# Token rows that hold the last 64 normalised channels once

## The reference

```
h = concat(patches @ W.T + b, txt)           # (32, 274, 192)
h = h + attention(layernorm(h))              # 12 heads of 16, rope, causal
x = layernorm(h)
route_c, route_u = argmax(softmax(x @ Wsc)), argmax(softmax(x @ Wsu))
out = h + ffn_common[route_c](x) + dropped * ffn_unique[route_u](x)
```

## Time and profile before

| | |
|---|---|
| median of 3 runs | 1414.29 us (1412.52 to 1417.49) |
| profiled execution | 1427.62 us, of which span 1425.9 us |
| attention phase | to about 925 us of the span |
| expert phase | from there, 44 tiles |
| busy in the span | PE 1234.0 us, PEld 1049.4, DVE 906.9, ACT 560.0, POOL 628.5 |
| moved | 177.93 MB, mean 125 GB/s |

### The profile page before, as it was taken

One profiled execution on the slowest core, in us unless ns is written; L12 is line 12 of the kernel. 1 busy time (PEld: TensorE's weight loads), 2 busy tenths in 40 slices (PEclk: granted clock), 3 DMA queues, 4 the chain that ended last, 5 costly groups with the idle time before them and its releaser, 6 DMA issues.

```text
span 1425.9 us, 33277 instructions
## 1 busy us (share of the span) xinstructions
PE 1234.0 (87%) x12722; PEld 1049.4 (74%) x12722; DVE 906.9 (64%) x2063; ACT 560.0 (39%) x959; POOL 628.5 (44%) x996
## 2 busy tenths in 40 slices
PE   6889999999999999999999987468995788889874
PEld 4667777777777777777777775367994787789874
DVE  5676776786787777787777874567873343445331
ACT  1234334434444344344344343133552344455430
POOL 4133333334534534534534525415325465455564
PEclk8899999999999999999999998579996899889987
DMA  6001211213323313213323223477764566657530
GB/s 204 20 20 48 69 39 58 63 58 100 111 60 107 106 58 111 99 61 104 108 59 106 86 61 109 144 292 271 254 236 126 168 213 208 220 207 271 203 127 26
DMA packets 84368, 177.93 MB, mean 125 GB/s; under 512 B 16446, under 2 KB 57701, under 8 KB 84208
## 3 DMA queue, kind: packets, MB, share of 16 engines
q1 hardware_dynamic: 70544, 146.93, 31.8%
q0 software_dynamic: 13664, 28.84, 5.7%
HBM read 129.15 MB, written 50.38 MB: 126 GB/s over the span
## 4 chain that ended last, share of the span: by engine, by line
PE 41%; DVE 21%; issue 15%; POOL 11%; ACT 6%; DMA 3%; another core or an unknown queue 1%; SPq 1%; POOLq 0%; DVEq 0%; ACTq 0%
PE y_ps L1629 9%; PE h_ps L1618 9%; DVE capped L971 4%; ACT PT L739 3%; PE round_banks L582 3%; PE gen L502 3%; POOL sorted_d L226 3%; DVE xn L987 3%; POOL PT L853 3%; PE gen L544 2%; PE round_banks L555 2%; DVE nm L975 2%; PE gen L511 2%; DVE nm L973 2%; PE gen L594 2%
## 5 line engine op out<-in xcount | busy, mean ns | idle before, releaser
L739 ACT ACTIVATE PT<-round_banks 128x1752 f32<-128x1752 f32 x96 | 156.7, 1632 | 176.0 <-PE round_banks L582 176.0
L853 POOL TENSOR_SCALAR_AFFINE_SELECT PT<-PT 128x512 f32<-128x512 f32 x192 | 118.1, 640 | 209.8 <-ACT PT L739 209.3
L1708 ACT ACTIVATE Gl<-h_ps,W 128x256 f32<-128x256 f32 x264 | 118.1, 474 | 233.1 <-PE h_ps L1618 147.8
L1618 PE MATMUL h_ps<-XH,Wh 128*128 128x256 f32 x528 | 155.4, 310 | 46.7 <-issue 29.9
L1629 PE MATMUL y_ps<-W,Gl 128*128 128x192 f32 x1056 | 193.2, 338 | 2.8 <-issue 2.8
L1629 PEld LDWEIGHTS y_ps<-W,Gl 128*128 128x128 f32 x1056 | 181.5, 199 | 4.9 <-issue 4.8
L1533 POOL DMA_INDIRECT out_dram<-Y,sid x88 | 95.5, 1085 | 154.3 <-DVE Y L1801 130.8
L502 PE MATMUL gen<-w_emb,xT 128*128 128x192 f32 (+1 forms) x768 | 142.9, 338 | 7.7 <-DMA ident<-in_ident_dram 7.7
L1618 PEld LDWEIGHTS h_ps<-XH,Wh 128*128 128x128 f32 x528 | 109.2, 207 | 50.9 <-issue 37.4
L1618 PE MATMUL h_ps<-XH,Wl 128*128 128x256 f32 x528 | 146.6, 297 | 0.0
L971 DVE TENSOR_TENSOR capped<-round_banks,masks_f 128x1024 f32<-128x1024 f32 x96 | 116.2, 1211 | 33.7 <-PE round_banks L555 33.7
(11 more groups left out here) (272 smaller groups left out, 2462.5 us busy)
## 6 DMA issues: line engine op xcount, KB each, us to landing
W<-in_experts_dram SPq DMA_DIRECT2D x44, 771.0 KB
W<-in_experts_dram SPq DMA_DIRECT2D x44, 672.0 KB
xT<-in_xT_dram SPq DMA_DIRECT2D x32, 591.0 KB
X<-sorted_d SPq DMA_DIRECT2D x35, 450.0 KB
stage<-rows_d SPq DMA_DIRECT2D x64, 224.0 KB
rows_d<-xn SPq DMA_DIRECT2D x32, 256.0 KB
rows_d<-h SPq DMA_DIRECT2D x32, 192.0 KB
out_dram<-h SPq DMA_DIRECT2D x32, 192.0 KB
```

The costliest lines, as they stand in the source:

```text
L739: act.activation(PT[(JG * b + j) % 2][:], R[:, :, 0:438], ACT.Exp, scale=SCALE).then_inc(exps, 1)
L853: pool.affine_select(x[:, :, at:at + P], x[:, :, at:at + P], [[0, GH], [1, P]], ALU.is_ge, 0.0, base=0, channel_multiplier=-1)
L1618: mm = pe.matmul(h_ps[f % 3][:, 0:ROWS], w[t.par][:, cols], x, start=(k == 0), stop=(k == len(products) - 1))
L1708: act.activation(Gl[t.par][:, f, :], h_ps[f % 3][:, 0:ROWS], ACT.Gelu, bias=W[t.i][:, B1O + f:B1O + f + 1]).then_inc(g_ready, 1)
```

## The change

The row of `rows_d` and `sorted_d` holds the 192 normalised channels once, 1544 bytes in all. VectorE writes them with one scaling per tile. In the expert phase TensorE turns columns 0 to 127 and then 64 to 191, so the second half of `xt_ps` has channels 64 to 127 in lanes 0 to 63 and channels 128 to 191 in lanes 64 to 127. ScalarE rounds all of it as before. VectorE takes the rest of lanes 64 to 127 and writes it to lanes 0 to 63 of XH, over the channels that are not needed. The high part is now in the upper lanes and the low part in the lower ones; the weights, being stored twice, are unchanged.

```diff
-DX = 2 * P
+DX = D
...
-            def scale_twice(which, k, dst, src):
-
-                scale(which, k, dst[:, 0:P], src[:, 0:P])
-                twice = lambda x: x.rearrange("p (a d) -> p a d", d=D - P)
-                return scale(which, k, twice(dst[:, P:DX]), twice(src[:, P:D]).broadcast_to([P, 2, D - P]))
...
-                    scale_twice(LN2, 0, xn2[b % 2][:, 0, :], h[b % 8][:, 0, :])
-                    scale_twice(LN2, 1, xn2[b % 2][:, 1, :], h[b % 8][:, 1, :]).then_inc(xn2_ready, 1)
+                    scale(LN2, 0, xn2[b % 2][:, 0, :], h[b % 8][:, 0, :])
+                    scale(LN2, 1, xn2[b % 2][:, 1, :], h[b % 8][:, 1, :]).then_inc(xn2_ready, 1)
...
-                    scale_twice(LN2T, 0, xn2t[:], ht[g % 4][:]).then_inc(xn2t_ready, 1)
+                    scale(LN2T, 0, xn2t[:], ht[g % 4][:]).then_inc(xn2t_ready, 1)
...
-                    mm = pe.transpose(xt_ps[:, ROWS + k * P:ROWS + (k + 1) * P],
-                                      x[:, k, P:DX], eye[:])
+                    mm = pe.transpose(xt_ps[:, ROWS + k * P:ROWS + (k + 1) * P], x[:, k, D - P:D], eye[:])
...
-                low, cols = slice(D - P, P), slice(ROWS, 2 * ROWS)
-                dve.tensor_tensor(XH[t.par][low, cols], xt_ps[low, cols], XH[t.par][low, cols], ALU.subtract).then_inc(xt_ready, 1)
+                low, high, cols = slice(0, D - P), slice(D - P, P), slice(ROWS, 2 * ROWS)
+                dve.tensor_tensor(XH[t.par][low, cols], xt_ps[high, cols], XH[t.par][high, cols], ALU.subtract).then_inc(xt_ready, 1)
```

## The result

The changed kernel took 1409.65 us (median of 20 runs, 1394.36 to 1420.93) against 1418.97 us before (20 runs, 1412.32 to 1426.71). The ratio is 0.9919, with a 95% interval of 0.9891 to 0.9947: 0.81% or 11.5 us faster, by the interval 7.5 to 15.5 us. The two medians are 9.3 us apart, and so are the means of all twenty; 11.5 us is the upper reading of the gain. The forecast was 1409.2 us, but it stood on three runs of before with a median of 1414.29 us, 4.7 us under that of the twenty. So the time was met partly by luck; what has to be judged is the difference. Forecast were 5.1 us, and measured were 9.3 or 11.5, about twice as much.

A forecast was written before the change was run, and what follows sets the result against it. TensorE was taken to bound the attention phase, VectorE's chain of waits the first 65 us of the expert phase. 3.5 + 1.1 + 0.5 = 5.1 us off 1414.29 gave 1409.2 us, range 1402 to 1418.

The forecast's parts named there:

- The fourth turns: Attention turns 8, 12 to 32, scalings beside GpSimd's selects: 0.5 us saved in each of seven, 3.5 us.
- The last turns: End of attention phase, no new batch: two lone scaling groups save 0.50 and 0.44 us, the tail 0.2; 1.1 us.
- The bytes: Four chained transfers between the phases, 13.5 us: rows of 1544 instead of 1800 bytes save 0.5 us.
- Covered after all: Rival, 21%: in attention, another wait replaces TensorE's 0.89 us and transfers are pure latency; gain 0 to 2.5 us, 1413 us.
- Fewer pauses: Rival, 16%: in the tile loop, 64 KB less per tile removes one or two pauses of 6.3 us; 1403 us.
- Other pauses: Rival, 16%: VectorE's program, 72 instructions shorter, shifts tile-loop pauses; slower from two more on, 1421.8 us.
- A second pass: Rival, 5%: L1770's write across lanes in the expert phase takes 850 ns, not 427; +5.6 us, 1414.8 us.
- The pair ahead of the selects: Fourth turns: scalings run before GpSimd's selects, take 0.67 us and save 1.2 us a turn, 8.5 us in seven; 1404.2 us.

The follow-up runs named there:

- before again: The kernel before, unaltered, run against itself: 1422.29 us, ratio 0.9977.
- short rows, old scalings: The changed kernel with 1544-byte rows kept but the two or four 128-column scalings of before: 1420.15 us, ratio 0.9994 to the kernel before.
- lanes alone: The kernel before with only the low half's lanes changed (reads lanes 64 to 127, writes 0 to 63): 1417.69 us, ratio 1.003.
- changed again: The changed kernel once more, no edit, against the kernel before: 1404.57 us, ratio 0.987.
- changed, third group: The changed kernel, unaltered, measured again in a later set of runs beside the kernel before: 1417.97 us, ratio 0.9958.
- third group: Last set of follow-up runs, on one chip, where the kernel before had a median of 1423.67 us.
- long rows, single scalings: The changed kernel with rows as long as before (256 columns, 64 of them zeros): 1410.08 us, ratio 0.991 to the kernel before.
- the two mixed kernels: Short rows; single scalings only in turns 8, 12 to 32, or everywhere but there: 1355.82 and 1357.9 us, ratios 0.9961 and 0.9968 to the kernel before.
- fillers: The changed kernel plus 72 short VectorE memsets, restoring the instruction count of before: 1359.19 us, ratio 0.9983; repeated, 1417.25 us, 0.9936 (to the kernel before).
- late selects: The changed kernel with GpSimd's first-third selects waiting until xn2 is written: 1352.96 us, ratio 0.9946; repeated, 1413.32 us, 0.9931 (to the kernel before).
- second group: Middle set of follow-up runs, on one chip, where the kernel before had a median of 1360.89 us.
- the complement: Short rows, single scalings everywhere but in turns 8, 12 to 32, which keep the old ones: 1357.9 us, ratio 0.9968 to the kernel before.

## Why the size was wrong

Counted from the first exponential of the attention phase (L739) to the first gelu of the tile loop, the profiles fall into two sets:

| profile | first L739 | last L739 | first gelu | first to first | gelu: first to last |
|---|---|---|---|---|---|
| before | 66.7 | 886.9 | 940.2 | 873.5 us | 458.2 us |
| before again | 65.2 | 885.5 | 938.6 | 873.4 | 454.5 |
| short rows, old scalings | 66.7 | 886.8 | 939.8 | 873.1 | 454.6 |
| lanes alone | 68.2 | 889.4 | 941.3 | 873.1 | 447.9 |
| changed | 64.3 | 876.8 | 927.9 | 863.6 | 452.3 |
| changed again | 64.2 | 876.8 | 927.8 | 863.6 | 435.6 |
| changed, third group | 66.5 | 880.7 | 932.2 | 865.7 | 458.3 |
| long rows, single scalings | 67.1 | 880.6 | 933.2 | 866.1 | 440.9 |

The mean of the upper four is 873.3 us, that of the lower four 864.8 us. They are 8.5 us apart (7.0 to 9.9 by single profiles). Two of the lower four (changed, changed again) also lack a stretch at half clock near 85 us, ahead of the first scaling of xn2, where the work is the same; it takes 1.5 us in the others. Without it the gain of the single scalings up to the first gelu is some 7.8 us, where the sum had 5.1. It divides so.

**The fourth turns: right.** The group is 1.89 - 1.43 = 0.46 us shorter, 0.5 forecast. The steps of L739 from one batch to the next are shorter by 0.56 and 0.64 us in turns 8 and 12 and by 0.45 to 0.47 in four others. In turn 24, the one from which the prediction read its wait, it is only 0.17 us: L971 starts 0.18 us after VectorE was free, for nothing that the profile names, and TensorE still waits 0.73 us. That is 3.2 us in the seven. Turns 15, 21 and 31 shift by 0.3 us each, two of them the wrong way: together 2.9 us, forecast 3.5.

**The last turns: nearly right.** The two lone groups take 0.67 us each instead of 1.17 and 1.11, which gives 0.9 us. The tail's takes 0.37 instead of 0.60, and TensorE's wait of 0.24 us is gone in turn 33. But the step of L739 there is 22.8 us in both kernels, so that this 0.2 us did not reach the end. 1.1 us were forecast.

**The bytes: 0 instead of 0.5 us.** 13.47 us for the four transfers against 13.48, and no gain of short over long rows. In the third group the four took 13.96 us in the changed kernel and 13.22 us in the one before, so what 14% fewer bytes are worth is less than what executions differ by.

**What was missing from the sum: the clock.** Nothing in the prediction priced what a lower granted clock in the attention phase costs or that the change could touch it. It makes itself felt in three places.

*First place, between 300 and 800 us.* All four profiles with the old scalings have a stretch at half clock (1.2 GHz) between 300 and 800 us, the two mixed kernels as well (near 686 and 477 us). Of the eight profiles with single scalings throughout, with fillers and late selects among them, only one has (late selects, third group). TensorE in such a stretch, from the timeline of the kernel before:

```profile
583.21 1.66 PE L544 MATMUL gen<-ident,rr 128*128 128x128 f32 x8
584.66 0.42 PE L702 MATMUL gen<-ident,nm 128*128 128x128 f32 x1
585.01 2.03 PE L582 MATMUL round_banks<-QKT 32*128 32x274 f32 x24
```

and at the same place of the changed kernel (third group):

```profile
581.03 1.10 PE L544 MATMUL gen<-ident,rr 128*128 128x128 f32 x8
581.97 0.27 PE L702 MATMUL gen<-ident,nm 128*128 128x128 f32 x1
582.17 1.12 PE L582 MATMUL round_banks<-QKT 32*128 32x274 f32 x24
```

The same 33 products take 1.80 us from start to start of the last plus 2.03, against 1.14 plus 1.12: 1.6 us.

*Second place, near 880 us.* This stretch stands behind a wait of TensorE of 1.75 us for L739. It is in the four profiles with the old scalings and in that with single scalings in the fourth turns only. It is in one of the eight others (fillers, second group), and not in the complement. TensorE there, from the timeline of the kernel before:

```profile
879.10 1.12 PE L582 MATMUL round_banks<-QKT 32*128 32x274 f32 x24 [1.75 <-ACT PT L739]
880.16 1.27 PE L609 MATMUL gen<-ident,Usb 128*128 128x128 f32 x6
...
882.21 1.63 PE L594 MATMUL gen<-PT,V 128*32 128x274 f32 x16
```

and from that of the changed kernel (third group):

```profile
874.55 1.12 PE L582 MATMUL round_banks<-QKT 32*128 32x274 f32 x24 [1.75 <-ACT PT L739]
875.60 0.88 PE L609 MATMUL gen<-ident,Usb 128*128 128x128 f32 x6
...
876.85 0.92 PE L594 MATMUL gen<-PT,V 128*32 128x274 f32 x16
```

It is worth another 1.6 us: VectorE's L1204 behind it comes 8.36 us after the last batch's first L739 in the kernel before, and 6.79 us in the changed one. It may not simply have gone, though. Every profile has another stretch at half clock some 20 us earlier, and in the seven of the eight that lack the one near 880 us this earlier one is longer than in the kernel before. From 845 to 870 us (us, PE, PEld, DVE, ACT, POOL, PEclk, DMA share, GB/s), before and changed (third group):

```profile
845.00:870.00 25.00, 18.84 (x277) 15.54 (x277) 17.09 (x42) 9.39 (x13) 9.81 (x19) 0.86 0.28 88
...
845.00:870.00 25.00, 19.41 (x283) 14.89 (x282) 15.51 (x30) 8.57 (x13) 10.51 (x21) 0.80 0.24 77
```

The clock is 0.80 there instead of 0.86, which is some 3 us more at half clock. The step of L739 around it is 22.8 us in both. So the time at half clock may in part have moved to a place where it costs less; that is a reading of the profiles, and no run tested it.

*Third place, the last batch's routing.* The long stretch at half clock that ends the attention phase begins 16.7 us after the last batch's first L739 in the kernel before, and 20.9 us after it in the changed one (third group). TensorE's work between the last two scaling groups falls into it in the first case (kernel before):

```profile
894.24 1.09 PE L511 MATMUL gen<-ident,xn 128*96 128x128 f32 x4 [1.64 <-DVE xn L987]
...
900.24 0.85 PE L527 MATMUL gen<-w_o,attT 96*128 96x192 f32 x2
```

and ahead of it in the second (changed, third group):

```profile
887.61 0.64 PE L511 MATMUL gen<-ident,xn 128*96 128x128 f32 x4 [1.13 <-DVE xn L987]
...
891.17 0.49 PE L527 MATMUL gen<-w_o,attT 96*128 96x192 f32 x2
```

The two scaling groups start 10.85 us apart before and 8.85 us after. Of these 2.0 us the shorter scaling is 0.5, and the clock 1.5. This one follows the change less closely than the others: three of the four profiles with the old scalings have the long distance (lanes alone has 9.35 us), and two of the eight with single ones (10.36 us in long rows and in late selects, third group).

The two profiles of the third group that differ by 7.7 us (873.4 to 865.7) then add up as follows: 2.9 (turns) + 1.6 (first place) + 1.6 (second) + 0.5 and 0.4 (lone scalings) + 1.5 (third) - 0.8 = 7.7 us. The -0.8 us lies behind the last tail, where the changed kernel was slower in this execution, 0.7 us of it in the four transfers. So the clock makes 4.7 us of it and the scalings themselves 3.8. The first profile of the changed kernel and its repetition have another 2.1 us, 1.5 of them because they also lack the half clock near 85 us (from the first L739 of batch 0 to that of batch 4 they take 101.5 instead of 103.0 us), which is no gain of the change.

**What is shown and what is argued.** Shown is that with the old scalings the first two stretches are there in every profile (the first at places that move between executions of one program, 583 and 316 us), and that with single scalings they are mostly absent; and what one costs. That is one profile of each run, four against eight. That the shorter waits of TensorE (0.43 instead of 0.89 us) keep the clock up is the natural reading, but it is argued: right ahead of the stretch at 583 us the two kernels show the same waits (0.38 us for L903). Two kernels speak against it: with single scalings in the fourth turns only, the wait is 0.43 us as well, and yet there is a stretch near 686 us; and with late selects it is gone in most fourth turns, and yet the third group's profile has a stretch near 475 us. The 1.75 us before the stretch near 880 us are the same in both kernels, too, so a wait by itself doesn't bring it down. Where in time a wait falls may matter, which no run tested. So why the clock is kept stays open.

**The rest, between 7.8 us and the 9.3 us of the medians or the 11.5 us of the ratio**, lies inside the interval and inside the tile loop's scatter. The changed kernel's three comparisons gave 0.9919, 0.987 and 0.9958. The last column of the table shows why: one and the same program has 435.6, 452.3 and 458.3 us there.

**The rivals.** *Covered after all* is refuted by the wait of 0.43 us and the steps. *Fewer pauses*, by fewer bytes, is not borne out: the long rows keep the gain. *Other pauses*, by a shifted program, is not borne out by the fillers of the third group, nor by the two profiles of the changed kernel, whose pauses differ though the program is the same; the fillers of the second group leave it some room. Its first price was also added up wrongly: one more pause of 6.3 us gives 1409.2 + 6.3 = 1415.5 us and not 1410.4. *A second pass* is refuted by 426 ns. The pair ahead of the selects did not come by itself, but the late selects show what it is worth against the kernel before, 0.46 + 0.48 = 0.94 us a turn and not the 1.2 us of the prediction: VectorE then waits for L502, and TensorE no longer for L973.

**In short.** The scalings' terms came nearly as summed (3.8 us of 4.6), the bytes gave nothing, and what made the gain larger is a term that the sum did not have. That the time of 1409.2 us was met rests on a low starting value and this missing term offsetting each other.

## What to carry to other kernels

Price a shorter instruction by the wait behind it and not by its busy time: here 0.5 us were worth nothing in the ordinary turns, where VectorE then waits for TensorE, and 0.46 us in each turn where it doesn't. When TensorE runs in long stretches at full clock with single short ones at half, put a term into the sum for those stretches, with a row that shows what one costs, and take it into the upper bound of the gain, since here it came to more than the counted terms (4.7 against 3.8 us). Two instructions of 192 columns have a quarter fewer columns than four of 128 and took 0.67 instead of 1.17 us. In the tails one wide instruction takes 0.37 us and two narrow ones 0.60, so a further wide one adds 0.30 us and a further narrow one just under 0.29: their count weighs more than their columns. And an order by which they don't meet GpSimd's selects is worth a further 0.76 us on VectorE, of which 0.48 us reached the end.

## What the runs showed of the hardware

**The pauses in the middle of the tile loop went with the chip.** In the second group none of the four kernels had them in 16 tiles in a row, while every profile of the other groups had. Some longer tiles before and behind these are there on every chip. The kernel with fillers, from 1050 to 1250 us, on the chip of the second group:

```profile
1050.00:1250.00 200.00, 190.83 (x1366) 190.36 (x1365) 101.86 (x188) 107.75 (x214) 140.50 (x160) 0.97 0.78 248
```

and the same program on the chip of the third:

```profile
1050.00:1250.00 200.00, 159.21 (x1038) 154.31 (x1037) 80.50 (x154) 81.85 (x161) 115.11 (x124) 0.89 0.59 193
```

A tile took 7.94 or 7.95 us in these 16 tiles, and the span was 1351.9 us instead of 1413.2. The DMA engines moved more in the fast case, 248 instead of 193 GB/s, so a high rate alone does not bring the pauses. What does was not looked for.

**An operation that reads lanes 64 to 127 and writes lanes 0 to 63** costs what one in place costs, 426 against 427 ns. By the Trainium skill (VectorE: DVE Perf Modes, Two Vector instructions with no wait between them) an operand that starts in another group of 32 lanes holds the instruction until the earlier ones are done; the runs agree in so far as nothing was added to a hold that was there already.

**The selects of GpSimd against VectorE's scalings.** Beside two selects (1.23 us) two scalings take 1.43 us instead of 0.67, four 1.89 instead of 1.17 or 1.11. The Trainium skill (SBUF — State Buffer, Who interferes with whom) describes such a lock on a shared port pair; with the selects behind the scalings it was gone.
